# Query items stored in memory by column of head, and the third chunk's keys and values projected in the first third of step 1

## The reference, cut to what matters

```python
x = hidden_states                       # (2, 1024, 512) f32
h = layernorm(x)
qkv = h @ Wqkv                          # 32 heads of 16 columns of q; one head of k and v, shared by all
scores = q k^T / 4 + slope_h * (pos_k - pos_q), causal
x = x + softmax(scores) v @ Wo
y = layernorm(x)                        # FFN: base matmul + top-2 of 8 low-rank experts
x = x + y @ W_base^T + b + sum_e route_w[e] * (y A_e^T) B_e^T
```

## Time and profile before

| | |
|---|---|
| median of three runs | 699.22 us (697.58 to 699.97) |
| the profiled execution | 698.62 us, span of its instructions 696.9 us |
| busy TensorE / VectorE / ScalarE / GpSimd | 673.5 / 552.3 / 360.7 / 216.5 us |
| granted TensorE clock | 0.999 of full speed |
| first slot of step 0 | at 31.44 us |
| steps 1 to 3 (from one slot 41 to the next) | 34.2, 34.2 and 33.9 us |
| query stores and loads | 16 DMAs of 384 KB, 96 of 128 KB |

### The profile page before, as it was taken

How to read it: one execution, slowest core, us unless ns; L and a number is a source line. 1 busy time by engine, 2 the same in 40 slices (tenths; PEclk the granted TensorE clock), 3 DMA queues, 4 the chain that set the end, 5 groups by cost and what they waited for, 6 DMA issues and landing times.

```text
span 696.9 us, 13297 instructions
## 1 busy us (share of the span) xinstructions
PE 673.5 (97%) x4326; PEld 308.8 (44%) x4326; DVE 552.3 (79%) x1794; ACT 360.7 (52%) x519; POOL 216.5 (31%) x366
## 2 busy tenths in 40 slices
PE   7899999999999999999999999999999999999997
PEld 5444344544454444435443343343333455555553
DVE  6798989787989889898988989989881375656565
ACT  3325656666657667666666666666668411111111
POOL 0054323233341614234252231422431412222220
PEclk9999999999999999999999999999999999999999
DMA  9778108081411443080144843325200189600001
GB/s 243 161 146 141 42 6 143 28 153 27 152 61 44 65 85 118 2 132 34 40 70 89 117 75 67 52 46 95 48 18 34 64 123 177 151 31 31 30 31 60
DMA packets 43000, 56.32 MB, mean 81 GB/s; under 512 B 6697, under 2 KB 26281, under 8 KB 42801
## 3 DMA queue, kind: packets, MB, share of 16 engines
q1 hardware_dynamic: 40344, 51.27, 37.1%
q10 hardware_dynamic: 2592, 4.26, 1.8%
HBM read 35.72 MB, written 19.79 MB: 80 GB/s over the span
## 4 chain that ended last, share of the span: by engine, by line
PE 83%; DVE 9%; DMA 2%; ACT 2%; issue 1%; SPq 1%; POOL 0%; DVEq 0%; ACTq 0%; POOLq 0%
PE psum L784 20%; PE psum L736 18%; PE psum L766 13%; PE psum L812 8%; PE psum L834 7%; PE psum L682 7%; PE psum L763 5%; DVE psum L1170 3%; PE psum L829 2%; PE psum L844 2%; ACT work L976 2%; DVE negm L1175 1%; DMA x_sb<-in_x 1%; PE psum L821 1%; DMA arena<-q_dram 1%
## 5 line engine op out<-in xcount | busy, mean ns | idle before, releaser
L976 ACT ACTIVATE work<-psum 128x1024 f32<-128x1024 f32 (+1 forms) x320 | 288.9, 942 | 125.1 <-PE psum L766 106.6
L1170 DVE CUSTOM_DVE_ANT_0 psum<-psum,future 128x384 f32<-128x384 f32 (+3 forms) x512 | 238.0, 514 | 14.9 <-PE psum L736 12.8
L736 PE MATMUL psum<-k_op,arena 106*128 106x512 bf16 (+3 forms) x768 | 212.2, 328 | 9.3 <-DVE negm L1170 3.1
L1175 DVE TENSOR_REDUCE negm<-psum 128x1 f32<-128x512 f32 x256 | 168.7, 688 | 15.4 <-PE psum L736 11.2
L1345 POOL TENSOR_SCALAR_AFFINE_SELECT work<-work 128x512 f32<-128x512 f32 x128 | 81.5, 637 | 296.8 <-ACT work L976 296.8
L784 PE MATMUL psum<-work,v_op 128*32 128x512 f32 (+3 forms) x1536 | 163.4, 498 | 0.6 <-POOL work L1345 0.4
L766 PE MATMUL psum<-arena,k_op 109*128 109x512 bf16 (+3 forms) x640 | 157.4, 316 | 1.0 <-ACT work L976 0.8
L736 PEld LDWEIGHTS psum<-k_op,arena 106*128 106x128 bf16 x768 | 69.1, 97 | 127.9 <-DVE negm L1170 39.7
L682 PE MATMUL psum<-arena,wqkv_sb 128*128 128x256 f32 (+3 forms) x240 | 84.5, 452 | 1.2 <-ACT arena L894 1.2
L763 PE MATMUL psum<-arena,k_op 116*128 116x128 bf16 x512 | 84.1, 221 | 0.9 <-ACT work L976 0.9
L766 PEld LDWEIGHTS psum<-arena,k_op 109*128 109x128 bf16 x640 | 59.6, 98 | 43.1 <-ACT work L976 14.7
(11 more groups left out here) (90 smaller groups left out, 456.1 us busy)
## 6 DMA issues: line engine op xcount, KB each, us to landing
arena<-q_dram SPq DMA_DIRECT2D x96, 128.0 KB, 5.4
o_dram<-o_sb SPq DMA_DIRECT2D x32, 256.0 KB
q_dram<-arena SPq DMA_DIRECT2D x16, 384.0 KB, 4.4
arena<-o_dram SPq DMA_DIRECT2D x32, 128.0 KB, 4.5
arena<-rcp_dram SPq DMA_DIRECT2D x32, 128.0 KB, 4.8
out<-wqkv_sb ACTq DMA_DIRECT2D x16, 256.0 KB, 2.0
work<-in_x SPq DMA_DIRECT2D x3, 1024.0 KB, 16.9
x_sb<-in_x SPq DMA_DIRECT2D x8, 256.0 KB, 5.1
```

What stands on the lines that cost most here:

```text
L736: last = nc.tensor.matmul(bank[:, a * width:(a + 1) * width], q_op[0:ROW_MAX, bass.ds(col, P)], k_op[0:ROW_MAX, b, k0:k0 + width], start=T ...
L976: nc.scalar.activation(probs[:, n % 4, heads * hp:heads * (hp + 1), 0:w], src, ACT.Exp).then_inc(exp_done, 1)
L1170: last = nc.vector.tensor_tensor_reduce(keys, keys, future[:, CH - width:CH], -1.0, 3e38, ALU.add, ALU.min, negm[:, late, 0, j * QT + t:j ...
L1175: nc.vector.tensor_reduce(dst, psum[:, bank, 0:len(js) * width].rearrange("p (a k) -> p a k", a=len(js)), AX_X, ALU.max, negate=True).then ...
```

## The change

Three edits. `q_dram` gets the axes (chunk, part, item, column of head, head, query). A store becomes three DMAs, one a part; the first waits for the first part alone, the other two for the split. A load then reads 16 rows of 8 KB without a gap. And in step 1 side uses are put in three times as early.

```diff
+SIDES_SOONER = {1: 3}
...
-        while side and (piece is None or (beside + sum(use_parts(side[0])) / 2) * whole <= done * extra):
+        while side and (piece is None or (beside + sum(use_parts(side[0])) / 2) * whole <= done * extra * SIDES_SOONER.get(k, 1)):
...
-        q_dram = nc.dram_tensor("q_dram", (NCH, 3, D, CH), BF16, kind="Internal").ap()
+        q_dram = nc.dram_tensor("q_dram", (NCH, 3, PAIRS, DH, 2 * UH, CH), BF16, kind="Internal").ap()
...
                 c, m = Q_ITEMS[n]
-                if n < 2:
-                    sp.wait_ge(q_split_v, n + 1)
-                else:
-                    sp.wait_ge(q_split_p, n - 1)
                 if n:
 
-                    sp.wait_ge(q_stored, 16 * n)
-                sp.dma_start(q_dram[c, :, P * m:P * (m + 1)].rearrange("a r q -> r a q"),
-                             qpart[:, n % 4]).then_inc(q_stored, 16)
+                    sp.wait_ge(q_stored, 48 * n)
+                sp.wait_ge(q_hi_ready, n + 1)
+                for a in range(3):
+                    if a == 1:
+                        if n < 2:
+                            sp.wait_ge(q_split_v, n + 1)
+                        else:
+                            sp.wait_ge(q_split_p, n - 1)
+                    sp.dma_start(q_dram[c, a, m].rearrange("d h q -> h d q"), qpart[:, n % 4, a]).then_inc(q_stored, 16)
...
-                    sp.dma_start(q_op_pairs[DH * r:DH * (r + 1), c % 2, g].rearrange("d (h q) -> d h q", q=CH),
-                                 q_dram[c, a, g * P:(g + 1) * P].rearrange("(h d) q -> d h q", d=DH)).then_inc(q_in[n % 2], 16)
+                    sp.dma_start(q_op_pairs[DH * r:DH * (r + 1), c % 2, g],
+                                 q_dram[c, a, g].rearrange("d h q -> d (h q)")).then_inc(q_in[n % 2], 16)
```

More of the change, by code:

```diff
@@ L481, in store_queries @@
                 c, m = Q_ITEMS[n]
-                if n < 2:
-                    sp.wait_ge(q_split_v, n + 1)
-                else:
-                    sp.wait_ge(q_split_p, n - 1)
                 if n:
-                    sp.wait_ge(q_stored, 16 * n)
-                sp.dma_start(q_dram[c, :, P * m:P * (m + 1)].rearrange("a r q -> r a q"),
-                             qpart[:, n % 4]).then_inc(q_stored, 16)
+                    sp.wait_ge(q_stored, 48 * n)
[7 more added lines that the diff above has]
+                    sp.dma_start(q_dram[c, a, m].rearrange("d h q -> h d q"), qpart[:, n % 4, a]).then_inc(q_stored, 16)
             def load_queries(n):
                 c, g = Q_ITEMS[n]
-                sp.wait_ge(q_stored, 16 * (n + 1))
+                sp.wait_ge(q_stored, 48 * (n + 1))
                 if n >= 2:
@@ L910, in query_hi @@
                 if n >= 4:
-                    act.wait_ge(q_stored, 16 * (n - 3))
+                    act.wait_ge(q_stored, 48 * (n - 3))
                 act.wait_ge(side_free, u + 1)
```

## The result

| | before | after |
|---|---|---|
| median | 699.38 us (697.51 to 699.97, 6 runs) | 704.44 us (702.69 to 705.03, 6 runs) |
| profiled execution, span | 698.62, 696.9 us | 704.49, 702.7 us |
| mean granted TensorE clock | 0.999 | 0.995 |
| step 1 (slot 41 to slot 41) | 34.2 us | 102.55 - 63.84 = 38.7 us |
| row of maxima in step 1: store, load issued | 67.12, 69.50 | 70.93, 74.00 |

The changed kernel is slower: ratio 1.008, 95% interval 1.0066 to 1.0093. That is above the range on record (698.9 to 703.5 us). The sign, slower, was the likeliest case of the forecast; the size was twice what was forecast (5.1 us by the medians, 5.6 by the ratio, for 2.7).

What follows compares the result with a forecast made beforehand. VectorE was taken to pace step 1, TensorE the steps from 2 on. The sum was 698.62 + 2.7 (step 1) + 0 (start) = 701.3 us, 701.9 against the median; forecast from 698.9: 701.6 us, range 698.9 to 703.5.

Steps and rivals of the forecast that it cites:

- The sign, slower: Whole kernel: slower by over 0.3%, chance 0.57, against 0.39 for within and 0.04 for faster.
- The mechanism: Step 1: 4,096 columns of attention fall behind slot 20, so VectorE's Newton steps wait for ScalarE's 1/sqrt guess, 3.1 us late.
- `scores(4, 1)` starts at about 79.75: TensorE in step 1, behind slot 20; a chain of 4.34 us from there puts the Newton steps at 84.1.
- a wait of about 3.5 us: VectorE in step 1, before the Newton steps: its wait for ScalarE's guess grows from 0.62 us to about 3.5 us.
- the late row: SyncE in step 1: extra query stores make the row of maxima 0.8 to 3.5 us later, nearly all hidden.
- no long wait for the guess: Rival, step 1: VectorE's wait stays under 1 us, -1.1 to +0.3 us, about 698.5 with faster loads; chance 0.10.
- Some is given back: with TensorE ahead, the 0.49 us at 94.60 goes: VectorE late in step 1: an idle gap vanishes, turning 3.1 us into 3.1 - 0.45 = 2.7 us net.
- until slot 24 finds no bank; then it stands, too: TensorE in step 1: runs ahead while VectorE waits, then stands before slot 24; no cost was given for it.
- `scores(4, 0)` moves from 71.5 to about 74, so it is hidden by nearly all of that.: TensorE in step 1: the scores needing the maxima move later, covering nearly all of the row's 0.8 to 3.5 us delay.
- up to 2 us: Step 1: cost of the later row of maxima if the factor's move did not cover it.
- So the loads start between 0.6 us earlier and 0.6 us later; I take 0.: Start of the kernel, item 0: the new query stores change when its loads begin by 0 us.
- My rival for it: Stores on half the DMA engines and a slower start: first slot at 32.0, +3.3 us, 702.2; chance 0.10.

Runs made afterwards that it cites:

- sooner_only: The kernel before with only the planner's factor 3 for step 1, layout and stores as before: 703.59 us, ratio 1.0062.
- full_rows: The whole change with the row of maxima of step 1 put ahead of the stores of items 4 and 5: 704.3 us, ratio 1.0072 to before.
- sooner_guess: The kernel before with factor 3 and ScalarE's 1/sqrt guess for chunk 3 moved behind the first exponentials of tile 4: 697.90 us, ratio 0.9988.
- full_guess: The whole change with ScalarE's 1/sqrt guess moved behind the first exponentials of tile 4: 699.49 us, ratio 1.0007 to the kernel before.
- sooner_rows_guess: The kernel before with factor 3, the 1/sqrt guess moved earlier and the row of maxima ahead of the stores, old layout: 698.31 us, ratio 0.9994.
- before_rows_guess: The kernel before with the 1/sqrt guess and the row of maxima moved earlier, old layout, no factor: 698.2 us, ratio 0.998.
- before_guess: The kernel before with only the 1/sqrt guess moved behind the first exponentials of tile 4: 698.76 us, ratio 0.9999.
- layout_only: The change without the planner's factor, so only the new query layout with three stores an item: 705.28 us, ratio 1.0086 to before.

## Why the prediction was wrong

**The mechanism was right.** Slots are placed by all work done, so `scores(5, 1)` fell behind slot 20, and the Newton steps waited for the guess behind it. Forecast: "`scores(4, 1)` starts at about 79.75", Newton steps at 84.1, a wait of about 3.5 us. Without the late row (sooner_only) they came at 84.63, which is 20.62 us after the end of step 0 against 17.28: +3.34 for the 3.1 forecast, and a wait of 3.44. `scores(4, 1)` started 16.29 us after the end of step 0 (80.30 - 64.01) for 16.06 forecast, and the chain behind it took 4.33 us for 4.34. Moving the guess took the wait away. The rival "no long wait for the guess" is out.

**Steps that failed:**

1. *"Some is given back: with TensorE ahead, the 0.49 us at 94.60 goes"*, -0.45. From the Newton steps to the turn it took 0.65 us more instead. This is the step that broke the forecast first. I let TensorE stand ("until slot 24 finds no bank; then it stands, too") and gave the standing no price. It stood for 2.88 us, and then it was at 0.64 and 0.51 of its clock for the four us from 88. Sooner_only, full_rows and the change, which have the wait, need 17.44, 17.54 and 17.53 us from there to the turn; sooner_guess and full_guess, with the same order on TensorE and no wait, 16.62 and 16.63. That is 0.9 us. So the new order gives back 0.26 us of the 16.88 of before, not 0.45, and the stall takes 0.9. In the change VectorE waits for TensorE at 90.95 and 93.01 (0.39 and 0.32 us), in and right behind the slow stretch, and sooner_guess has neither wait. The second drop at 388 adds 1.18 us and was no term of the forecast either; it is in three of the six traces with the new layout, and in none of the seven with the old one. What brings it on there is open: TensorE stands 1.3 us before the same slot in all thirteen.
2. *"`scores(4, 0)` moves from 71.5 to about 74, so it is hidden by nearly all of that."* I had the load of the maxima 0.8 to 3.5 us later; it was 4.5. The stores of item 4 began 1.26 us later (62.17 for 60.91), the two items held the queue for 8.76 us instead of 6.21 (six issues of 0.58 us instead of two of 0.38, and each item waited for at the lower rate), and the row's load followed its store by 3.07 us instead of 2.38, with the bulk of item 5 still moving; in full_rows, with nothing ahead, it followed by 1.92. The cover was short by 1.28 us on TensorE, 0.55 us in the end; with the early guess it was enough. That it would cost "up to 2 us" without this cover was the worst miss: it cost 4.02 us of waiting, and 5.8 us with the clock.
3. *"So the loads start between 0.6 us earlier and 0.6 us later; I take 0."* The new stores move 186 GB/s at a DMA share of 0.53, those of the earlier trace rows 248 at 0.72, three separate ones in the old shape 285 at 0.87. GB/s by share are 351, 344 and 328: what is busy works as fast as before, and less of it is busy. In this one execution the start was even (31.21 for 31.44, loads issued at 23.30 for 23.12), but by chance: from the split on, the loads came 0.95 us later than in the kernel before, and 1.1 us later on average over the traces. In the ratios the layout without its late row costs 0.8 to 1.4 us, most of it here. The Trainium skill gives a reason why such a store would be slow ("DMA: Bandwidth & Descriptors", section on why a DMA increments its semaphore by 16: the engines are the largest number up to 16 that divides the outer sizes, here 8); by it the share of a store alone could be at most a half. The share of 0.53 with some other traffic, and the old shape at 0.87, agree; how many engines a store used no view shows, and no run has the outer size without the rows 8 KB apart. My rival for it had the slower store, but at +0.6 us for the start, and nothing for the row behind the stores.

**What held.** The query loads gained next to nothing: 131 GB/s at full share with rows of 8 KB, 121 with rows of 1 KB, and from the first load to the first slot 0.1 us less, although the page counts 32375 packets instead of 43000. The list of VectorE's idle times left out 0.38 us at 77.49, which changes nothing in the sum. Steps 2 and on kept their lengths up to 380 us. The move of the keys and values brings nothing by itself: with the guess early, the kernel with the factor (sooner_rows_guess, 0.9994) and without it (before_rows_guess, 0.998) have overlapping intervals, sooner_guess (0.9988) and before_guess (0.9999) stand the other way round, and in the traces step 1 is 33.7 us long with it and 33.5 without.

**The sum**, forecast and measured: start 0, 0.15 (about 1 on average); the wait 3.1, 3.34; the late row 0, 0.56; given back -0.45, +0.65; a second stretch at the lower clock, not forecast, 1.18; the rest -0.1. Together 2.7 and 5.8 us.

**The version to keep** is the kernel before with the guess and the row of maxima moved: 698.2 us, ratio 0.998 [0.9963, 0.9996], step 1 at 33.45 us. The gain is 1.4 us by the ratio, with an interval from 0.3 to 2.6. sooner_guess (0.9988) can't be told from it, and neither can before_guess, whose step 1 is as short (33.46 us); that the row's move adds anything there is not shown.

## What to carry to other kernels

When a planner's weights are changed, look for the steps on other engines that are tied to a number in the list (here "behind slot 20" and "behind tile 5") and check that they still stand in the same order; a line moved by about one tile was worth 4 to 5 us here, and the factor that made it necessary nothing. Price a stall of TensorE of about 3 us at more than its length, since the clock may be lower behind it. And before a bulk store is given a new shape, look at what short, urgent transfer stands behind it in the same queue, and at the outer size of the shape.

## What the runs showed of the hardware that was not expected

- The five longest stalls of TensorE in the thirteen traces (from 5 us on) all went with work at the lower clock: 2.68 us idle, then 0.50 and 0.78 (full_guess, at the start), 2.88 us idle, then 0.64 and 0.51 from 88 to 92 (the change), 2.88 and 0.58, 0.56 (sooner_only), 2.88 and 0.87, 0.50, 0.78 (full_rows), 4.02 and 0.50 (layout_only). A shorter stall did it only at times: in all thirteen traces TensorE stands 1.3 us before the same slot near 385, and the clock falls behind it in three. The slot in the change, where the clock fell, then in the kernel before, where it did not, with the stretch that follows (columns as in the earlier trace rows):

```profile
387.89 0.39 PE L739 MATMUL psum<-k_op,arena 106*128 106x256 bf16 x2 [1.32 <-DVE negm L1173]
...
383.19 0.39 PE L736 MATMUL psum<-k_op,arena 106*128 106x256 bf16 x2 [1.32 <-DVE negm L1170]
...
384.00:386.00 2.00, 2.00 (x24) 1.15 (x21) 2.00 (x10) 1.09 (x2) 0.00 (x0) 1.00 0.07 16
```

- A store of 128 KB written as 8 x 16 rows of 1 KB took 0.58 us to issue against 0.42 for 128 rows of 1 KB, stretches of such stores show about half of the DMA engines' time used (0.53), and from the stores of two parts to the first load it took 3.4 to 4.3 us, against 2.5 to 2.9 with the old stores.
- A load into 16 partitions goes at 120 to 150 GB/s at a full DMA share, whether its rows are 1 or 8 KB (121 and 135 with 1 KB in two stretches of the kernel before; 131 in the change, 139 and 148 in layout_only, with 8 KB).
- The first slot started between 30.25 and 33.76 us over thirteen executions of nearly the same beginning. A change of 1 us in front of step 0 can't be read from one trace.
